# One core, attention and experts over 32 sequences: producers moved ahead in each slot, value matmuls in two bursts, values and gates in one float32 matmul, a straight program for the first sequences

## The chip, the cores and the metric

The kernel runs on one core of a Trainium2 chip. The core has five engines that run their own programs side by side and wait for each other on semaphores: TensorE (PE; its weight load is PEld), VectorE (DVE), ScalarE (ACT), GpSimd (POOL) and SyncE (SP), which here issues every DMA. The metric is the device time of one launch in microseconds (us). A run is called by its median over several executions; the profile is one further execution.

## The reference

`x` is 32 sequences of 256 tokens with 128 features. The result is `x + attention(layernorm(x)) + experts(layernorm(x))`.

```
xn = (x - mean) / sqrt(var + 1e-5)
q, k, v = xn @ Wq.T + bq, xn @ Wk.T + bk, xn @ Wv.T + bv      # 16 heads of 8 features
scores = q k^T / sqrt(8), causal;  attn = softmax(scores);  a = (attn v) @ Wo.T + bo
logits = xn @ gate_w.T                                        # 8 experts
top 2 of 8, softmax of the two logits; y = sum of the two experts xn @ We[e], weighted
out = x + a + y
```

## The kernel before

The unit of work is one sequence. The work on a sequence is spread over six slots of the program. Slot `s` holds, in every engine's program, the work of several sequences at once, each at another stage: sequence `s+3` (`NXT`) is normalised, turned by TensorE and split into a high and a low half in `fp32r`; sequence `s+2` (`PRE`) is projected to q and k, and each of these is split into three bf16 parts; sequence `s` has its scores taken; sequence `s-1` has its transposed scores, exponentials and experts; sequence `s-2` is finished. Each slot has 12 items `n` (`ITEMS`); each item is one 128x512 block of scores of sequence `s` on TensorE, whose row maxima VectorE takes (`take_max`, L589), and one 128x512 block of transposed scores (`scoreT_item`) of the sequence that is one slot behind for n of 4 and more (`LAG`), two behind for n under 4, whose exponentials ScalarE takes (L473). Both have two PSUM buffers: block n waits for the reader of block n-2.

The three bf16 parts travel over DRAM: SP writes them to `scratch` (L305 to L309) and loads them back as rows of `qstack` and `kstack` (L323, L327), 1.2 MB a sequence in six DMAs. The row maxima travel too: TensorE turns them (L914), ScalarE and VectorE split them (L518, L633, `mT`), and SP writes them as two rows of `qstack` (L299). The first transposed block of a sequence, at n = 4 of the next slot, waits for these two rows (`dma_max`). The other rows of a stack are constants (`q_steps`, `k_steps`), filled once for each of the four buffers by VectorE (L737) and ScalarE (L554).

Values and gates: `m1 = xnT.T @ wvg` at n = 0, as four products of halves for each of the two 128-token tiles (`by_halves(..., whole=True)`, eight matmuls of 136 columns). Experts: four blocks of three matmuls with 512 columns (L779), at n = 4, 6, 8 and 10, in two PSUM tiles `m1` and `m2`, read by VectorE (`lower`, L626) and ScalarE (`upper`, L508). Attention values (`values`, L847): four groups a sequence, at n = 9 and 11 of slot `s+1` and n = 3 and 5 of slot `s+2`, from two `probs` buffers. An fp32 matmul stands in the trace as two records.

The order of the work is written out by hand, by `if n == ...` in each engine's `slot`. `over_slots` runs slots -3 to 3 straight, 4 to 27 in a loop of four, and the rest straight; `between(s)` is what the start does between two slots (filling constants, splitting weights). SP issues its DMAs in program order, and a wait holds back all that stands behind it.

Of the kernel before, what the change touches and what calls it, by code (L numbers as in the profile page):

```python
# [33 lines left out]
E = 8  # L34
# [80 lines left out]
def bass_block(nc, x, wq, wk, bq, bk, wv, bv, wo, bo, gate, we, out):  # L115
    ctx = ExitStack()
    with ctx:
# [12 lines left out]
        def sems(*names):  # L130
# [8 lines left out]
        wvg_hl = sb("wvg_hl", [P, 2, VG], FP32R)  # L139
# [6 lines left out]
        ident_b = sb("ident_b", [P, P], BF16)  # L146
# [8 lines left out]
        xb = sbs("xb", [P, QT, D])  # L155
        xnT_hl = sbs("xnT_hl", [P, 2, S], FP32R)
# [6 lines left out]
        probs = sbs("probs", [P, 3, HG, P], n=2)  # L163
# [8 lines left out]
        wvg_high = sb("wvg_high", [P, VG])  # L172
# [38 lines left out]
        ld_qk, ld_w, ld_we, ld_bias, pool_const, dve_const, pe_bias, dve_bias = sems(  # L211
            "ld_qk", "ld_w", "ld_we", "ld_bias", "pool_const", "dve_const", "pe_bias", "dve_bias")
# [8 lines left out]
        pe_xnT, dve_halves, act_high, pool_xb = sems("pe_xnT", "dve_halves", "act_high", "pool_xb")  # L221
# [11 lines left out]
        NQK, NW, CONSTS = 4, 4, 8  # L233
# [6 lines left out]
        def over_slots(eng_fori, slot, between=None):  # L240

            for s in range(-NXT, LOOP0):
                slot(Seq(0, s), s)
                if between:
                    between(s)
# [19 lines left out]
        def _(sp):  # L265
# [3 lines left out]
            sp.dma_start(bqk_sb[:, 0:1], bq.unsqueeze(1)).then_inc(ld_qk, 16)  # L269
            sp.dma_start(bqk_sb[:, 1:2], bk.unsqueeze(1)).then_inc(ld_qk, 16)  # L270
            sp.dma_start(wvg_sb[:, 0:D], wv).then_inc(ld_w, 16)
            sp.dma_start(wvg_sb[:, D:VG], gate).then_inc(ld_w, 16)
            sp.dma_start(wo_sb[:], wo).then_inc(ld_w, 16)
            sp.dma_start(bv_sb[:], bv.unsqueeze(1)).then_inc(ld_w, 16)
            sp.dma_start(bias_out[:], bo.unsqueeze(0).to_broadcast([P, D])).then_inc(ld_bias, 16)
# [7 lines left out]

            def slot(t, s):
                if has(s, -3):
                    store(t + (-3))
                if has(s, NXT) and s > -NXT:
                    nxt = t + NXT
                    sp.wait_ge(pool_xn, upto(nxt + (-NB)))
                    sp.wait_ge(pool_xb, upto(nxt + (-NB)))  # L290
                    sp.dma_start(x_sb[nxt.buf][:], x_t[nxt.n]).then_inc(dma_x[nxt.buf], 16)
                if s == -2:
                    sp.dma_start(we_sb[:], we.rearrange("e d m -> d e m")).then_inc(ld_we, 16)
# [705 lines left out]
```

## Time and profile before

| | us |
|---|---|
| three runs, median (lowest, highest) | 561.86 (561.7, 562.83) |
| the profiled execution, its own time | 564.58 |
| its span, first to last instruction | 562.8 |
| PE busy | 516.0 |
| DVE busy | 439.1 |
| ACT busy | 400.9 |
| POOL busy | 346.4 |

The span splits in three: a start up to the first full slot, thirty slots of nearly one length, and a tail in which no new sequence comes. Busy PE is not PE at its peak; the chain of waits shows the distance from one piece of PE work to the next. The granted TensorE clock stands in tenths of full speed; its mean over the execution is 0.993.

### The profile page before, as it was taken

The numbers are of one execution on the slowest core, as the hardware profiler recorded it, in microseconds if no ns is written. First come the engines' busy times: TensorE is split into PE (matmuls) and PEld (weight loads), VectorE is DVE, ScalarE is ACT, GpSimd is POOL, SyncE is SP. The second block draws the span as 40 slices with busy tenths as digits, with TensorE's granted clock in tenths as the row PEclk, the third lists the DMA queues.
The fourth block names the chain that finished last, engine by engine and source line by source line (L and its number), as shares of the span: only waits on it lengthen the run. The fifth ranks groups of instructions, "written<-read, shape, count | busy, mean of one in ns | idle before, by whom it ended". The sixth has DMA issues, their size and how long they took to land.

```text
span 562.8 us, 19500 instructions
## 1 busy us (share of the span) xinstructions
PE 516.0 (92%) x6402; PEld 402.3 (71%) x6402; DVE 439.1 (78%) x1109; ACT 400.9 (71%) x1033; POOL 346.4 (62%) x565
## 2 busy tenths in 40 slices
PE   1157999999999999999999999999999999999986
PEld 1145777777777777777777787777777778777754
DVE  3268888888888888888888888888888888877721
ACT  5624677777777777778777777777877777776664
POOL 4323576666666777666666677766666667754433
PEclk9999999999999999999999999999999999999988
DMA  3645555464455555544544555554445455540000
GB/s 98 172 98 139 137 138 137 110 145 125 110 132 137 145 137 135 134 130 120 128 128 117 137 145 136 131 139 126 128 118 133 115 139 147 137 130 12 12 12 20
DMA packets 64002, 67.11 MB, mean 119 GB/s; under 512 B 6752, under 2 KB 59104, under 8 KB 59104
## 3 DMA queue, kind: packets, MB, share of 16 engines
q1 hardware_dynamic: 63968, 66.68, 47.0%
q8 instruction: 19, 0.31, 0.2%
q14 instruction: 15, 0.12, 0.1%
HBM read 44.90 MB, written 21.23 MB: 118 GB/s over the span
## 4 chain that ended last, share of the span: by engine, by line
PE 79%; ACT 7%; DMA 4%; issue 4%; DVE 3%; POOL 2%; SPq 1%; ACTq 1%; POOLq 0%; DVEq 0%
PE m L779 26%; PE oT_ps L847 14%; PE scoreT_ps L823 10%; PE score_ps L803 9%; PE scoreT_ps L828 6%; PE score_ps L797 4%; ACT probs L473 3%; PE m L956 3%; DMA qstack<-mT 2%; PE m L951 2%; ACT parts L496 2%; PE m L893 1%; PE m L925 1%; DMA x_sb<-in_x 1%; PE m L914 1%
## 5 line engine op out<-in xcount | busy, mean ns | idle before, releaser
L589 DVE TENSOR_REDUCE negmax<-score_ps 128x2 f32<-128x512 f32 (+1 forms) x384 | 260.4, 686 | 51.9 <-PE score_ps L803 37.8
L473 ACT ACTIVATE probs<-scoreT_ps 128x512 f32<-128x512 f32 x384 | 225.8, 607 | 88.7 <-PE scoreT_ps L823 44.5
L779 PE MATMUL m<-we_hl,xnT_hl 128*128 128x512 f32 x384 | 122.9, 429 | 0.0
L847 PE MATMUL oT_ps<-probs,vaug 128*32 128x256 f32 (+1 forms) x2048 | 110.2, 333 | 0.0
L823 PE MATMUL scoreT_ps<-qstack,kstack 123*128 123x128 bf16 (+1 forms) x1024 | 102.7, 222 | 5.1 <-DMA qstack<-mT 4.5
L803 PE MATMUL score_ps<-kstack,qstack 72*128 72x128 bf16 (+1 forms) x1024 | 104.3, 224 | 1.9 <-DVE negmax L589 1.8
L372 POOL TENSOR_TENSOR fours<-lower,upper 128x512 f32<-128x512 f32 x64 | 81.8, 1278 | 22.1 <-ACT upper L508 21.3
L823 PEld LDWEIGHTS scoreT_ps<-qstack,kstack 123*128 123x128 bf16 (+1 forms) x1024 | 68.3, 98 | 33.1 <-issue 21.6
L366 POOL TENSOR_TENSOR parts<-rest,parts 128x256 bf16<-128x256 f32 x64 | 41.9, 673 | 72.0 <-ACT parts L501 71.6
L847 PEld LDWEIGHTS oT_ps<-probs,vaug 128*32 128x32 f32 x2048 | 53.6, 109 | 37.6 <-issue 5.4
L803 PEld LDWEIGHTS score_ps<-kstack,qstack 72*128 72x128 bf16 (+1 forms) x1024 | 71.1, 100 | 5.6 <-DVE negmax L589 3.8
L508 ACT ACTIVATE upper<-m,weight 128x128 f32<-128x128 f32 x256 | 73.5, 381 | 0.0
L779 PEld LDWEIGHTS m<-we_hl,xnT_hl 128*128 128x128 f32 x384 | 63.8, 193 | 5.7
L432 POOL TENSOR_SCALAR xn<-x_sb,mv,rstd 128x128 f32<-128x128 f32 x64 | 51.0, 802 | 8.1 <-POOL rstd L427 8.1
L828 PE MATMUL scoreT_ps<-qstack,kstack 123*128 123x128 bf16 x512 | 50.9, 222 | 3.6 <-ACT probs L473 1.8
L797 PE MATMUL score_ps<-kstack,qstack 123*128 123x128 bf16 x512 | 51.5, 224 | 0.5 <-DVE negmax L589 0.5
L828 PEld LDWEIGHTS scoreT_ps<-qstack,kstack 123*128 123x128 bf16 x512 | 29.2, 98 | 27.2 <-issue 15.0
L379 POOL TENSOR_TENSOR gap<-top 128x2 f32<-128x2 f32 x32 | 6.3, 196 | 66.6 <-DVE top L598 66.6
L626 DVE TENSOR_TENSOR lower<-m,weight 128x512 f32<-128x512 f32 x64 | 43.6, 681 | 4.7 <-PE m L779 4.7
L496 ACT ACTIVATE parts<-m,bqk_sb 128x256 bf16<-128x256 f32 x64 | 26.9, 471 | 22.4 <-PE m L779 22.4
L416 POOL TENSOR_TENSOR pairs<-fours 128x512 f32<-128x512 f32 x32 | 41.0, 1283 | 0.2
L797 PEld LDWEIGHTS score_ps<-kstack,qstack 123*128 123x128 bf16 x512 | 35.5, 100 | 7.5 <-DVE negmax L589 7.0
(82 smaller groups left out, 696.6 us busy)
## 6 DMA issues: line engine op xcount, KB each, us to landing
kstack<-scratch SPq DMA_DIRECT2D x96, 192.0 KB
scratch<-parts SPq DMA_DIRECT2D x64, 192.0 KB, 2.4
qstack<-scratch SPq DMA_DIRECT2D x64, 192.0 KB
qstack<-scratch SPq DMA_DIRECT2D x32, 256.0 KB
x_sb<-in_x SPq DMA_DIRECT2D x32, 128.0 KB, 2.1
scratch<-parts SPq DMA_DIRECT2D x32, 128.0 KB, 1.9
out<-out_sb SPq DMA_DIRECT2D x32, 128.0 KB, 1.9
qstack<-mT SPq DMA_DIRECT2D x64, 8.0 KB, 1.8
```

The costliest lines, as they stand in the source:

```text
L372: g.tensor_tensor(fours[:, :, q, :], lower[:, :, q, :], upper[:, :, q, :], ALU.add).then_inc(pool_sum, 1)
L432: ins = g.tensor_scalar(xn[:, q, :], x_sb[nxt.buf][:, q, :], mv[:, q, 0:1], rstd[:, q:q + 1], ALU.subtract, ALU.mult)
L473: a.activation(o, i, ACT.Exp, scale=SCALE).then_inc(act_exp, 1)
L508: ins = a.activation(upper[:, e, q, :], m2[:, e * D:(e + 1) * D], ACT.Copy, scale=weight[m.buf][:, q, EH + e:EH + e + 1])
L589: v.tensor_reduce(o, score_ps[n % 2][:].rearrange("p (h k) -> p h k", h=w), axis=AX.X, op=ALU.max, negate=True).then_inc(dve_max, 1)
L626: v.tensor_tensor(lower[:, :, q, :], m1[:].rearrange("p (e m) -> p e m", e=EH), weight[m.buf][:, q, 0:EH].unsqueeze(2).to_broadcast([P, EH ...
L779: ins = tn.matmul(o, l, r, start=i == 0, stop=i == len(products) - 1)
L797: ins = tn.matmul(ps[:, c * P:(c + 1) * P], qs[0:ALL_ROWS, h, 0:P], ks[0:ALL_ROWS, h, 0:P], start=True, stop=True)
L803: ins = tn.matmul(ps[:, c * S + q * P:c * S + (q + 1) * P], qs[0:top, h, P:S], ks[0:top, h, q * P:(q + 1) * P], start=True, stop=True)
L823: ins = tn.matmul(ps[:, c * S + q * P:c * S + (q + 1) * P], ks[0:top, h, 0:P], qs[0:top, h, q * P:(q + 1) * P], start=True, stop=True)
L828: ins = tn.matmul(ps[:, c * P:(c + 1) * P], ks[0:ALL_ROWS, h, P:S], qs[0:ALL_ROWS, h, P:S], start=True, stop=True)
L847: ins = tn.matmul(o, va[:, q, h, :], i, start=q == 0 and grp % VGRP == 0, stop=q == 1 and grp % VGRP == VGRP - 1, skip_group_check=True)
```

## The change

The following changes, and nothing else:

- Values and gates become one fp32 matmul for each 128-token tile, from a plain fp32 copy `xnT` of the turned input. ScalarE makes this copy (`copy_input`) before VectorE splits the same PSUM tile. The split of `wvg` goes.
- The four groups of attention values move: groups 0 and 1 together at n = 3 of slot `s+2`, groups 2 and 3 together at n = 6. `probs` has four buffers for it.
- Expert blocks 0 and 1 stand together at n = 4, block 2 at n = 9, block 3 at n = 11. Values and gates move from n = 0 to n = 1.
- Many pieces on ACT, DVE and POOL change their item: the row statistics of `s+3` from n = 6 and 7 to n = 1 and 2, `xn` from 7 to 5, `oT` from 5 to 6, `part1` from n = 1 to 2, the two `upper` blocks in front of the item's exponential or behind it.
- SP loads the input four slots ahead, and behind the maxima instead of ahead of them.
- Slots -3 to -1 are replaced by a straight program for sequences 0 to 2 on each engine; x of the first four sequences is loaded at once. `ident_b`, which nothing read, goes.
- The constants of the stacks: `kstack` 0 is filled by VectorE, `kstack` 1 by ScalarE ahead of slot 0, `kstack` 2 and 3 behind slots 0 and 1. The experts' weights are split behind slot 0 instead of ahead of it.

```diff
+            for s in range(LOOP0):
                 slot(Seq(0, s), s)
                 if between:
...
+            sp.dma_start(x_sb[1][:], x_t[1]).then_inc(dma_x[1], 16)
+            sp.dma_start(bqk_sb[:, 0:1], bq.unsqueeze(1)).then_inc(ld_bqk, 16)
+            sp.dma_start(bqk_sb[:, 1:2], bk.unsqueeze(1)).then_inc(ld_bqk, 16)
...
+            sp.dma_start(bv_sb[:], bv.unsqueeze(1)).then_inc(ld_w, 16)
+            sp.dma_start(wo_sb[:], wo).then_inc(ld_w, 16)
+            sp.dma_start(x_sb[2][:], x_t[2]).then_inc(dma_x[2], 16)
+            sp.dma_start(wvg_sb[:, 0:D], wv).then_inc(ld_w, 16)
+            sp.dma_start(wvg_sb[:, D:VG], gate).then_inc(ld_w, 16)
+            sp.dma_start(bias_out[:], bo.unsqueeze(0).to_broadcast([P, D])).then_inc(ld_bias, 16)
+            sp.dma_start(we_sb[:], we.rearrange("e d m -> d e m")).then_inc(ld_we, 16)
+            sp.dma_start(x_sb[3][:], x_t[3]).then_inc(dma_x[3], 16)
...
+                if s + PRE < NB:
+
+                    sp.wait_ge(dve_stack, s + PRE + 2)
+                    sp.wait_ge(act_stack, s + PRE)
+                    sp.wait_ge(ld_zero, 16 * NB)
...
+                if has(s, NB):
+                    new = t + NB
+                    sp.wait_ge(pool_xn, upto(t))
+                    sp.wait_ge(pool_xb, upto(t))
+                    sp.dma_start(x_sb[new.buf][:], x_t[new.n]).then_inc(dma_x[new.buf], 16)
...
+            for s in range(-PRE, 0):
+                stacks(Seq(0, s + PRE), s)
...
+            normalise(Seq(0, 0))
+            mask_steps()
+            normalise(Seq(0, 1))
+            part3(Seq(0, 0))
+            normalise(Seq(0, 2))
+            part3(Seq(0, 1))
...
+                    act.wait_ge(pe_pv, upto(f + (-1), per=NG, k=grp + 1))
...
+            def copy_input(nxt):
+                act.wait_ge(pe_xnT, upto(nxt))
+                a.copy(xnT[nxt.buf][:], m1[:, 0:S]).then_inc(act_xnT, 1)
...
+                    if n == 11 and has(s, NXT):
+                        copy_input(t + NXT)
                     if n == 11 and has(s, -1):
-                        upper_experts(t + (-1), 1)
+                        upper_experts(mix, 1)
+                    if n == 11 and has(s, NXT):
...
             def between(s):
-                if s < NB - NXT:
-                    if s == -NXT:
-                        act.wait_ge(pool_steps, 2 * STEPS + 1)
-                    fill_keys(s + NXT)
-                if s == -1:
+                if s == 0:
                     act.wait_ge(dve_weights, 3)
-                    a.copy(wvg_hl[:, 0], wvg_high[:]).then_inc(act_weights, 1)
-                    act.wait_ge(dve_weights, 5)
                     a.copy(we_hl[:, 0], w_high[:]).then_inc(act_weights, 1)
+                if s < 2:
+                    fill_keys(s + 2)
...
+            copy_input(Seq(0, 0))
+            round_input(Seq(0, 0))
+            act.wait_ge(ld_bqk, 16 * 2)
+            part1(Seq(0, 0))
+            part2(Seq(0, 0))
+            copy_input(Seq(0, 1))
+            round_input(Seq(0, 1))
+            part1(Seq(0, 1))
+            part2(Seq(0, 1))
+            copy_input(Seq(0, 2))
+            round_input(Seq(0, 2))
+            act.wait_ge(pool_steps, 2 * STEPS + 1)
+            fill_keys(1)
             over_slots(act.Fori, slot, between)
 
...
+            fill_stack(qstack[0], q_steps)
+            fill_stack(kstack[0], k_steps)
+            take_rest(Seq(0, 1))
+            fill_stack(qstack[1], q_steps)
+            dve.wait_ge(pe_bias, 1)
...
-            def by_halves(o, high, low, other_high, other_low, whole=False):
-
-
-                products = [(high, other_high), (high, other_low), (low, other_high)] + [(low, other_low)] * whole
-                for i, (l, r) in enumerate(products):
-                    ins = tn.matmul(o, l, r, start=i == 0, stop=i == len(products) - 1)
+            def by_halves(o, high, low, other_high, other_low):
...
-                            ins = by_halves(m1[:, q * VG:(q + 1) * VG], xnT_hl[t.buf][:, 0, q * P:(q + 1) * P],
-                                            xnT_hl[t.buf][:, 1, q * P:(q + 1) * P], wvg_hl[:, 0], wvg_hl[:, 1], whole=True)
+                            ins = tn.matmul(m1[:, q * VG:(q + 1) * VG], xnT[t.buf][:, q * P:(q + 1) * P], wvg_sb[:],
+                                            start=True, stop=True)
...
-                    if n == 7 and has(s, -2):
+                        project(pre)
+                    if n == 3 and has(s, -2):
+                        values(fin, 0)
+                        values(fin, 1)
+                    if n == 4 and has(s, -1):
+                        if s == 1:
+                            pe.wait_ge(dve_weights, 4)
+                            pe.wait_ge(act_weights, 2)
+                        if has(s, 0):
+                            pe.wait_ge(act_v, upto(t))
+                        else:
+                            pe.wait_ge(dve_lower, upto(fin, per=2))
+                        experts(mix, 0)
+                        if has(s, PRE):
+                            pe.wait_ge(dve_rest, upto(pre, per=2))
+                        else:
+                            pe.wait_ge(act_upper, upto(fin, per=2))
+                        experts(mix, 1)
+                    if n == 6 and has(s, -2):
+                        values(fin, 2)
+                        values(fin, 3)
+                    if n == 8 and has(s, -2):
                         pe.wait_ge(act_oT, upto(fin))
...
+                    if n == 9 and has(s, -1):
+                        pe.wait_ge(dve_lower, upto(mix, per=2, k=1))
+                        experts(mix, 2)
...
+                    if n == 11 and has(s, -1):
+                        pe.wait_ge(act_upper, upto(mix, per=2, k=1))
+                        experts(mix, 3)
...
+            pe.wait_ge(pool_const, 5)
+            turn_input(Seq(0, 0))
+            pe.wait_ge(dve_weights, 2)
+            pe.wait_ge(act_weights, 1)
+            project(Seq(0, 0))
+            pe.wait_ge(dve_halves, 2)
+            turn_input(Seq(0, 1))
+            pe.wait_ge(ld_w, 16 * NW)
+            pe.wait_ge(dve_const, 1)
+            tn.matmul(m0[:, 0:D], bv_wide[:], wo_sb[:], start=True, stop=True).then_inc(pe_bias, 1)
+            project(Seq(0, 1))
+            pe.wait_ge(dve_halves, 4)
+            turn_input(Seq(0, 2))
+            over_slots(pe.Fori, slot, between=None)
 
```

TensorE, slot 2 before, from score block 3 to score block 6 (`score_ps` scores, `scoreT_ps` transposed scores, `oT_ps` attention values, `we_hl` experts):

```order
L797 MATMUL score_ps<-kstack,qstack 128x128 x4
L847 MATMUL oT_ps<-probs,vaug 32x256 x4
L847 MATMUL oT_ps<-probs,vaug 32x128 x4
L828 MATMUL scoreT_ps<-qstack,kstack 128x128 x4
L803 MATMUL score_ps<-kstack,qstack 128x128 x4
L779 MATMUL m<-we_hl,xnT_hl 128x512 x3
L823 MATMUL scoreT_ps<-qstack,kstack 128x128 x4
L803 MATMUL score_ps<-kstack,qstack 128x128 x4
L823 MATMUL scoreT_ps<-qstack,kstack 128x128 x4
L847 MATMUL oT_ps<-probs,vaug 32x256 x4
L847 MATMUL oT_ps<-probs,vaug 32x128 x4
L797 MATMUL score_ps<-kstack,qstack 128x128 x4
```

The same slot in the changed kernel, from score block 3 to the transposed block of n = 4:

```order
L829 MATMUL score_ps<-kstack,qstack 128x128 x4
L879 MATMUL oT_ps<-probs,vaug 32x256 x4
L879 MATMUL oT_ps<-probs,vaug 32x128 x4
L879 MATMUL oT_ps<-probs,vaug 32x256 x4
L879 MATMUL oT_ps<-probs,vaug 32x128 x4
L860 MATMUL scoreT_ps<-qstack,kstack 128x128 x4
L835 MATMUL score_ps<-kstack,qstack 128x128 x4
L811 MATMUL m<-we_hl,xnT_hl 128x512 x6
L855 MATMUL scoreT_ps<-qstack,kstack 128x128 x4
```

Two groups of values now stand between one score block and the next, and two expert blocks between the next two.

ScalarE, the end of slot 0 and the start of slot 1 in the changed kernel (`kstack<-k_steps` fills constants, `mT` is the split of the maxima, which SP sends on):

```order
L519 CAST xnT_hl<-xnT_high 128x256
L575 CAST we_hl<-w_high 128x1024
L569 COPY kstack<-k_steps 64x4096
L486 COPY logits<-m 128x16
L496 COPY vaug<-m 128x8x2x8 x2
L538 CAST mT<-m 16x256
```

The same place before:

```order
L554 COPY kstack<-k_steps 64x4096
L525 CAST xnT_hl<-xnT_high 128x256
L478 COPY logits<-m 128x16
L488 COPY vaug<-m 128x8x2x8 x2
L518 CAST mT<-m 16x256
```

The cast of the experts' weights and the fill of `kstack` 2 come between the last work of slot 0 and the maxima of sequence 0.

SyncE, slots 0 and 1 in the changed kernel (the loads of stack 2, the maxima of sequence 0, the input of sequence 5, the first parts of sequence 3):

```order
L309 DMA qstack<-scratch 24x4096 x2
L309 DMA qstack<-scratch 32x4096
L313 DMA kstack<-scratch 24x4096 x3
L324 DMA qstack<-mT 1x16x256 x2
L329 DMA x_sb<-in_x 128x2x128
L291 DMA scratch<-parts 128x2x256
```

The same place before:

```order
L323 DMA qstack<-scratch 24x4096 x2
L323 DMA qstack<-scratch 32x4096
L327 DMA kstack<-scratch 24x4096 x3
L291 DMA x_sb<-in_x 128x2x128
L299 DMA qstack<-mT 1x16x256 x2
L305 DMA scratch<-parts 128x2x256
```

Only the input moved behind the maxima. In both kernels the maxima of sequence 0 stand behind the loads of stack 2, and these wait for the fill of `kstack` 2. That fill stood before slot 0; now it is the one behind slot 0 on ScalarE.

## Rows read from the trace of the kernel before

**Rows 1.** The page: busy time by engine; the chain of waits by engine.

```profile
PE 516.0 (92%) x6402; PEld 402.3 (71%) x6402; DVE 439.1 (78%) x1109; ACT 400.9 (71%) x1033; POOL 346.4 (62%) x565
...
PE 79%; ACT 7%; DMA 4%; issue 4%; DVE 3%; POOL 2%; SPq 1%; ACTq 1%; POOLq 0%; DVEq 0%
```

**Rows 2.** Stretches: length, busy us of each engine, granted clock, DMA share, GB/s.

```profile
208.70:224.30 15.60, 15.52 (x202) 12.23 (x202) 13.29 (x35) 11.88 (x33) 10.69 (x18) 1.00 0.53 137
...
223.30:224.30 1.00, 1.00 (x14) 0.99 (x13) 0.53 (x2) 1.00 (x4) 0.79 (x2) 1.00 0.73 172
224.30:225.30 1.00, 1.00 (x13) 1.00 (x13) 0.85 (x2) 0.48 (x3) 1.00 (x1) 1.00 0.01 0
```

**Rows 3.** Chain of waits in one steady slot: start us, us, what.

```profile
208.45 0.23 PE score_ps L797 x4
208.67 0.90 PE m L779 x8
...
212.30 0.50 ACT probs L473
...
212.84 0.40 PE scoreT_ps L828 x4
...
214.48 0.23 PE score_ps L803 x4
...
214.94 0.79 PE oT_ps L847 x16
215.73 0.33 PE score_ps L797 x4
...
223.56 0.50 PE m L956 x4
224.06 0.22 PE score_ps L797 x4
```

**Rows 4.** Groups of instructions: busy us, mean ns, idle before and its releaser.

```profile
L589 DVE TENSOR_REDUCE negmax<-score_ps 128x2 f32<-128x512 f32 (+1 forms) x384 | 260.4, 686 | 51.9 <-PE score_ps L803 37.8 <-PE score_ps L797 8.2 <-issue 0.2
...
L554 ACT COPY kstack<-k_steps 64x4096 bf16<-64x4096 bf16 x4 | 14.4, 3602 | 0.1
...
L548 ACT COPY oTn<-m 128x256 f32<-128x256 f32 x32 | 11.7, 367 | 2.5 <-PE m L925 2.5
...
L737 DVE COPY qstack<-q_steps 64x4096 bf16<-64x4096 bf16 x4 | 4.9, 1224 | 0.1
...
L566 ACT CAST we_hl<-w_high 128x1024 fp32r<-128x1024 f32 x1 | 1.0, 1047 | 2.3 <-DVE w_high L643 2.3
```

**Rows 5.** Who waited for whom: us in total, times, longest.

```profile
PE scoreT_ps L823 <- DMA qstack<-mT: 4.5, 6, 1.3
PEld scoreT_ps L823 <- DMA qstack<-mT: 4.2, 13, 0.8
```

**Rows 6.** DMA issues: KB each, median us from issue to landing.

```profile
qstack<-mT SPq DMA_DIRECT2D x64, 8.0 KB, 1.8
```

**Rows 7.** Chain of waits at the start: an input issued behind six stack loads.

```profile
19.50 6.91 DMA x_sb<-in_x
```

**Rows 8.** Timeline of PE at the start (slot 0, slot 1, slot 2).

```profile
34.78 0.63 PE L797 MATMUL score_ps<-kstack,qstack 123*128 123x128 bf16 x4
...
57.16 0.65 PE L823 MATMUL scoreT_ps<-qstack,kstack 123*128 123x128 bf16 x4
...
66.44 0.39 PE L797 MATMUL score_ps<-kstack,qstack 123*128 123x128 bf16 x4
```

**Rows 9.** Timeline of DVE at the start (slot 0, slot 1).

```profile
37.33 1.28 DVE L589 TENSOR_REDUCE negmax<-score_ps 128x4 f32<-128x512 f32 x2
...
53.73 0.41 DVE L633 TENSOR_TENSOR mT<-m,mT 16x256 bf16<-16x256 f32 x1
```

**Rows 10.** Timeline of PE in the tail.

```profile
541.90 1.63 PE L779 MATMUL m<-we_hl,xnT_hl 128*128 128x512 f32 x3
...
545.47 0.95 PE L779 MATMUL m<-we_hl,xnT_hl 128*128 128x512 f32 x3
```

More of the change, by code:

```diff
@@ L446, in slot @@
                                         bias_out[:].unsqueeze(1).to_broadcast([P, QT, D]), ALU.add).then_inc(pool_xb, 1)
-                    if n == 10 and has(s, -1):
-                        sum_tile(t + (-1), 0)
+                    if n == 0 and has(s, -2):
+                        sum_tile(fin, 1)
+                    if n == 1 and has(s, -2):
+                        pool.wait_ge(pool_sum, upto(fin, per=RESULT, k=SUM_Q1))
+                        g.tensor_tensor(pairs[:], fours[:, 0:2], fours[:, 2:4], ALU.add).then_inc(pool_sum, 1)
@@ new lines, in slot @@
+                    if n == 2 and has(s, 0):
+                        gates(t, GAP)
+                    if n == 3 and has(s, -2):
+                        pool.wait_ge(pool_sum, upto(fin, per=RESULT, k=PAIRS))
+                        g.tensor_tensor(mixed[:], pairs[:, 0], pairs[:, 1], ALU.add).then_inc(pool_sum, 1)
+                    if n == 4 and has(s, PRE):
+                        part3(t + PRE)
+                    if n == 5 and has(s, -2):
+                        pool.wait_ge(pool_sum, upto(fin, per=RESULT, k=FOURS))
+                        pool.wait_ge(pool_xb, upto(fin))
+                        pool.wait_ge(dve_out, upto(fin + (-1)))
+                        g.tensor_tensor(res[:], mixed[:], xb[fin.buf][:], ALU.add).then_inc(pool_sum, 1)
@@ L667, in slot @@
+                    if n == 2 and has(s, 0):
                         best_experts(t)
                     if n == 2 and has(s, PRE):
[L669 to L674 removed]
+                        take_rest(t + PRE)
@@ L957, in slot @@
                         ins.then_inc(pe_y, 1)
-            def between(s):
-                if s == -1:
-                    pe.wait_ge(ld_w, 16 * NW)
-                    pe.wait_ge(dve_const, 1)
-                    tn.matmul(m0[:, 0:D], bv_wide[:], wo_sb[:], start=True, stop=True).then_inc(pe_bias, 1)
-            EXPERT_STEPS = (4, 6, 8, 10)
-            pe.wait_ge(pool_const, CONSTS + 2)
-            over_slots(pe.Fori, slot, between)
+                    if f:
+                        scoreT_item(f, k)
+                    if n == 10 and has(s, -2):
+                        pe.wait_ge(dve_o, upto(fin))
+                        for q in range(QT):
+                            ins = tn.transpose(m0[:, q * P:(q + 1) * P], o_sb[:, q, :], ident[:])
+                        ins.then_inc(pe_oTn, 1)
+            pe.wait_ge(pool_const, 5)
[12 more added lines that the diff above has]
+            over_slots(pe.Fori, slot, between=None)
 def kernel(L0_attn_x, L0_attn_Wq, L0_attn_bq, L0_attn_Wk, L0_attn_bk, L0_attn_Wv, L0_attn_bv,
```

491 lines of the change are left out of this document (210 added, 281 removed).

## The prediction

> **What bounds the kernel.** I read the page first: PE is busy for 92% of the span and makes 79% of the chain of waits [rows 1]. Then the stretches: in one steady slot PE is busy for 15.52 of 15.60 us, DVE for 13.29, ACT for 11.88, POOL for 10.69, at granted clock 1.00, the 2.4 GHz level [rows 2]. A busy PE may still stall inside, so I read the chain of one slot piece by piece. From score block 0 at 208.45 to the next slot's at 224.06 are 15.61 us, and the pieces follow each other with nothing between, save one place where the chain passes through an exponential at 212.30 and a transposed block takes 0.40 us instead of 0.24, a wait of some 0.15 us [rows 3]. So in thirty of the slots time is the sum of PE's pieces, and the change is worth there what it takes from that sum, as long as no other engine takes over. At the start PE mostly waits; what counts there is when each sequence's first piece can run, which the timelines tell [rows 7 to 9].
>
> **Values and gates.** Eight matmuls take 0.90 us of the chain from 208.67 [rows 3]. The two fp32 ones become four records of 136 columns. The nearest row is L956, four records of 128 columns: 0.50 us [rows 3], so 0.50 x 136/128 = 0.53, a gain of 0.37 us a slot. Best bound: four records at the pace of a 128-column score matmul (0.23/4) would take 0.25, gain 0.65. Worst: weight loads that are not hidden, 0.9 us or more, gain 0. I take 0.53, since L956 has the same types and nearly the same shape.
>
> The Trainium skill, Perfetto Trace Analysis (the table of engine rates), halves TensorE's output rate for FP32_LOW_HIGH, and its page TensorE: Matmul & The Clock Gate (weight-path perf modes) gives the fast weight load only to types other than FP32. By the rate alone four records of 136 columns would take 4 x 136 x 2 / 2.4 GHz = 0.45 us as an estimate; the L956 row gives 0.50 for 128, so the trace is a bit slower than that rule, and a penalty on the weight load, if there is one, is already in that row.
>
> **Bursts.** A score block costs 0.23 us of the chain, but 0.33 behind a group of values (215.73 against 214.48) [rows 3]. Four groups pay this before, two pairs now: gain 2 x 0.10 = 0.20 us a slot, between 0 (each group pays it by itself) and 0.35 (the entry into a group is cheaper too).
>
> **Pieces further from their producers.** The 0.15 us wait for the exponential behind `part1` should go. Blocks of transposed scores also wait for the maxima that come by DMA: 4.5 + 4.2 = 8.7 us in 19 waits [rows 5]. Experts 0 and 1 and the first pair of values now lie ahead of the block that waits, so it comes some 0.7 us later behind its producer than before. Of the 8.7 us I count 2.0 as gained in the steady part; PE and PEld may show one wait twice. The next slot's maxima go out about 0.9 us after the six loads of a stack are through; before, those loads end at about 224.3, where the DMA share falls from 0.73 to 0.01 [rows 2], so there is still room, but little.
>
> **What the cover must hold.** I added the engines' pieces in the new order over one slot. ACT gets one copy more, 0.37 us (like L548) [rows 4]: 12.3 of 15.0 us. DVE keeps its 13.3, so it may idle 1.7 us a slot. At four places the reader of a PE tile or its producer is within 0.1 us of being late: exponential 6 for block 8 (it stands behind `oT`), `oT` for its transposes, the lower experts' product for the turned input, `o_sb` for its transposes. I take 0.15 us a slot for these together. Zero is possible, and 0.5 if each of them pays 0.1 and drags the next.
>
> Slot: 0.37 + 0.20 + 0.15 - 0.15 = 0.57 us, 15.61 to 15.04. Thirty slots: 17.1, with the maxima 19.1 us.
>
> **The start.** The straight program has stack 0 ready to load at about 17.7 us, set by DVE, which now fills both its constants, 2 x 1.22 us [rows 4]. Loads take some 8 us. Before, score block 0 nevertheless came at 34.78 [rows 8], since the third input landed only 6.91 us after it was issued at 19.50, behind the six loads [rows 7], and weights were split ahead of the first row maxima at 37.33 [rows 9]. Now inputs are there early: score block 0 at about 26. That is 8.8 us ahead. But much of it is given back. DVE's slot 0 (10.5 us as before, and the `q` fill and the experts' weights behind it, 4 us) ends at 43. ACT waits for those weights, casts them (1.05) and fills `kstack` 2 (3.60) [rows 4], to 46.6. Then come the maxima of sequence 0: `mT` at 48 against 53.73 [rows 9]. The loads of stack 2 wait for the same fill and are issued from 46.7 to 49.0; SP issues the maxima only behind them. A DMA of maxima lands in 1.8 us [rows 6], but directly behind six loads an input took 6.91 [rows 7]. So the maxima land at about 55, and the first transposed block, with both expert blocks done, runs there. Before, it ran at 57.16 with one expert block still to come (1.4 us at the low clock) [rows 8]: 58.6 against 55.2, 3.4 us gained. The two groups of values that leave slot 1 give 1.6 more; a later warm-up of PE takes 1.0. Slot 1 ends 4.0 us ahead (66.44 [rows 8] becomes 62.4).
>
> Slot 2: `kstack` 3 is filled behind slot 1, 3.60 us on ACT [rows 4], when exponentials are due. ACT's queue behind it: an exponential, the logits, the maxima, `part1`. The fill ends 5.1 us into the slot; stack 3's six loads wait for it, and the maxima of sequence 1 stand behind them: they land at 5.1 + 8.5 = 13.6 us, where PE wants them at 6.9. That is 6.7 us of stall. In the tail before, three expert matmuls took 1.63 us behind such waits against 0.95 elsewhere [rows 10], so PE's clock falls back; I add 1.5 us. Loss in slot 2: 8.2. Start in sum: 4.0 - 8.2 = -4.2 us, a loss. Bounds: the maxima overtake the loads and the clock holds, +4.3; both stalls 2 us longer, -8.
>
> The Trainium skill, TensorE: Matmul & The Clock Gate (HAM oscillation), says that a long enough idle stretch throttles TensorE again; the tail row agrees with it.
>
> **The tail.** Values of the last sequence, two groups, move to after its last blocks: +2.1 us. The expert pair and the first pair of values fill the wait for the last maxima: -2.2. In sum 0, within 2 either way.
>
> **Sum.** 19.1 - 4.2 = 14.9 us. The profiled execution took 564.58 us, which becomes 549.7. The median of the runs is 561.86, 2.7 below; with the same saving it becomes 547.0.
>
> **Rivals.**
> 1. The maxima are not held by the loads (they share the queues fairly). For it: steady maxima land in 1.8 us while other traffic runs [rows 6]. Against it: the 6.91 us of [rows 7]. The start then gains 4.3: 561.86 - 19.1 - 4.3 = 538.5.
> 2. The near ties all pay: 0.5 us a slot in place of 0.15, and the maxima's 2 us are not gained. 547.0 + 30 x 0.35 = 557.5. For it: the bursts, 1.7 us in which no block comes, use up the two-buffer cushion. Against it: DVE idles 51.9 us before its maxima now [rows 4], so there is some slack.
> 3. DVE becomes the bound: slower. Mechanism: TensorE delivers score blocks in clumps. During each of the four bursts (two pairs of values, the expert pair, expert block 3 with the output product) DVE runs dry for 0.7 us, and its work cannot be made up. 13.3 us of DVE work plus 2.8 = 16.1 a slot, 0.5 more than now: 561.86 + 15 + 4.2 = 581. It decides once DVE idles more than 15.6 - 13.3 = 2.3 us a slot, which is just what it idles now [rows 2]. Against it: the present idle is time in which DVE waits for PE, not a need.
> 4. No gain: the fp32 matmuls cost the 0.90 of the eight and the bursts pay per group. The start's loss and small gains cancel: about 561.
>
> **Chances.** Forecast 0.55, with 542 to 551.5 as its own range. Rival 1 0.16, rival 2 0.18, rival 3 0.06, rival 4 0.05. The range 537 to 556.5 holds nearly all of the forecast, most of rival 1 and half of rival 2. A measurement of this kernel tells about 0.2% (1.1 us) from no change. Faster by more: 0.55 + 0.16 + 0.17 + 0.02 = 0.90; the same 0.03; slower 0.07.
>
> **What would show it.** Steady pitch of score block 0 at 15.04 us, values and gates 0.53, one 0.33 piece behind each pair of values. First row maxima near 27 us. The fill of `kstack` 2 ending near 46.6 and the first transposed block at about 55. In slot 2, a PE wait of over 5 us for `qstack<-mT`. Wrong if the pitch is over 15.3 (a near tie pays: the waits name which), if the maxima in slots 1 and 2 land in 2 us behind the loads, or if score block 0 is not before 30 us.

## The result, and the profile after

The kernel after takes 582.7 us (median of 4 runs, 576.1 to 588.3) against 562.35 beside it on the same chip: ratio 1.032, 95% interval 1.023 to 1.041. The run of 588.3 fell in a slower state and is left out of the ratio. The kernel is slower; forecast were 547.0 us, within 537.0 to 556.5, with a chance of 0.90 for faster. The profiled execution took 584.07 us, with a span of 582.3.

Its page, first the busy times, the granted clock of the 40 slices, the instruction queues and the chain by engine:

```profile
PE 499.8 (86%) x6274; PEld 408.2 (70%) x6274; DVE 426.1 (73%) x1108; ACT 403.3 (69%) x1063; POOL 349.0 (60%) x563
...
PEclk9965869999979999699988999699996999999999
...
q8 instruction: 64, 1.05, 0.8%
q14 instruction: 40, 0.33, 0.2%
...
PE 74%; issue 8%; DMA 6%; ACT 4%; DVE 4%; SPq 2%; POOL 1%; ACTq 0%; POOLq 0%; DVEq 0%
```

PE is busy for 16 us less than in [rows 1], yet the span is 19.5 us longer. "issue", time in which an engine waits for nothing that the profile shows, has 8% of the chain where [rows 1] have 4%, and the clock falls at regular places. In the kernel before q8 moved 19 packets and q14 15.

The steady slot answers to [rows 2, 3]. Windows (length, busy us of PE, PEld, DVE, ACT, POOL, granted clock, DMA share, GB/s), and some of the chain's pieces (start us, us, what):

```profile
138.39:152.85 14.46, 14.46 (x200) 12.05 (x204) 12.77 (x35) 12.02 (x34) 10.67 (x18) 1.00 0.56 138
...
229.60:234.63 5.03, 0.00 (x0) 0.00 (x1) 0.47 (x2) 1.37 (x5) 2.52 (x2) 0.79 0.42 91
235.88:238.08 2.20, 0.00 (x0) 0.00 (x1) 0.09 (x1) 0.42 (x1) 0.00 (x0) 0.50 0.00 0
238.08:244.93 6.85, 6.85 (x71) 5.86 (x72) 3.94 (x12) 2.89 (x9) 0.88 (x2) 0.66 0.09 25
```

```profile
138.39 1.44 PE oT_ps L879 x32
139.83 0.33 PE scoreT_ps L860 x4
...
150.47 0.52 PE m L919 x4
```

An undisturbed slot takes 14.46 us, less than the forecast 15.04. All of it is PE at the 2.4 GHz level. Values and gates take 0.52 us, a pair of values 1.44 and the block behind it 0.33. The windows below it show a disturbed slot. PE does nothing for 5.03 us, in which the others run out of work (POOL is still busy for 2.52 us, ACT for 1.37), and again for 2.20 us, in which all are nearly idle (ACT 0.42, DVE 0.09). Then come 6.85 us at a granted clock of 0.66, partly at the 1.2 GHz level. The chain shows this pattern five times, always ahead of score block 0 of the slot to which the loop branches back (slots 4 to 27 are six passes of four slots, so five branches back). These are its pieces "issue" of over 1 us, and below them PE's own waits (us in total, times, longest):

```profile
164.24 2.77 issue
167.75 2.40 issue
...
229.60 5.03 issue
235.88 2.20 issue
...
297.69 5.43 issue
304.36 1.92 issue
...
366.38 4.56 issue
372.18 1.62 issue
...
433.76 5.23 issue
440.24 1.64 issue
```

```profile
PE score_ps L829 <- issue: 23.0, 5, 5.4
...
PE score_ps L835 <- issue: 9.8, 5, 2.4
```

The start answers to [rows 8, 9]. Timelines of PE and of DVE, in brackets the wait:

```profile
27.12 0.59 PE L829 MATMUL score_ps<-kstack,qstack 123*128 123x128 bf16 x4 [6.87 <-DMA kstack<-scratch]
...
57.59 0.59 PE L855 MATMUL scoreT_ps<-qstack,kstack 123*128 123x128 bf16 x4 [4.53 <-DMA qstack<-mT]
...
64.91 0.39 PE L829 MATMUL score_ps<-kstack,qstack 123*128 123x128 bf16 x4
...
80.42 0.58 PE L855 MATMUL scoreT_ps<-qstack,kstack 123*128 123x128 bf16 x4 [3.66 <-DMA qstack<-mT]
```

```profile
27.74 1.29 DVE L612 TENSOR_REDUCE negmax<-score_ps 128x4 f32<-128x512 f32 x2 [4.83 <-PE score_ps L829]
...
48.72 0.41 DVE L707 TENSOR_TENSOR mT<-m,mT 16x256 bf16<-16x256 f32 x1 [2.65 <-ACT mT L538]
```

The chain of waits over the same time shows what the forecast named, the fills and the maxima behind them:

```profile
44.32 3.61 ACT kstack L569
...
51.03 6.43 DMA qstack<-mT
...
66.82 3.61 ACT kstack L569
...
73.75 6.53 DMA qstack<-mT
...
95.00 3.12 DMA qstack<-mT
```

Where the 19.5 us of span went can be read from the chain: values and gates of slot 4 start at 98.43 before and at 106.95 after (where they stand one score block and one transposed block, 0.45 us, later in the slot), those of slot 31 at 521.20 and at 545.63. So the start lost 8.1 us, the 27 slots between lost 438.7 - 422.8 = 15.9 us, and the end gained 4.5. At 14.46 a slot the 27 would have taken 390.4: the stalls cost 48 us and turned a gain of 32 into this loss.

### The profile page after: what moved, and what is told of

It is laid out like the page before. It is cut to its first block, busy times and chain, and to the rows that moved or that the text cites. A ratio compares the mean times of both kernels' runs of the same rounds, so it can differ in the third digit from the quotient of the medians.

```text
span 582.3 us, 19332 instructions
## 1 busy us (share of the span) xinstructions
PE 499.8 (86%) x6274; PEld 408.2 (70%) x6274; DVE 426.1 (73%) x1108; ACT 403.3 (69%) x1063; POOL 349.0 (60%) x563
## 3 DMA queue, kind: packets, MB, share of 16 engines
q8 instruction: 64, 1.05, 0.8%
## 4 chain that ended last, share of the span: by engine, by line
PE 74%; issue 8%; DMA 6%; ACT 4%; DVE 4%; SPq 2%; POOL 1%; ACTq 0%; POOLq 0%; DVEq 0%
PE m L811 18%; PE oT_ps L879 15%; PE scoreT_ps L855 10%; PE score_ps L835 10%; PE scoreT_ps L860 6%; PE score_ps L829 5%; DMA qstack<-mT 4%; PE m L919 3%; PE m L962 2%; PE m L980 2%; PE m L894 2%; DVE negmax L612 1%; ACT upper L526 1%; ACT kstack L569 1%; PE m L987 1%
## 5 line engine op out<-in xcount | busy, mean ns | idle before, releaser
L612 DVE TENSOR_REDUCE negmax<-score_ps 128x2 f32<-128x512 f32 (+1 forms) x384 | 251.1, 678 | 99.1 <-PE score_ps L835 70.1
L481 ACT ACTIVATE probs<-scoreT_ps 128x512 f32<-128x512 f32 x384 | 218.7, 603 | 115.9 <-PE scoreT_ps L860 64.7
L835 PE MATMUL score_ps<-kstack,qstack 72*128 72x128 bf16 (+1 forms) x1024 | 107.8, 228 | 19.4 <-issue 9.8
L811 PE MATMUL m<-we_hl,xnT_hl 128*128 128x512 f32 x384 | 114.7, 421 | 0.0
L879 PE MATMUL oT_ps<-probs,vaug 128*32 128x256 f32 (+1 forms) x2048 | 99.5, 336 | 0.0
L835 PEld LDWEIGHTS score_ps<-kstack,qstack 72*128 72x128 bf16 (+1 forms) x1024 | 74.3, 102 | 23.5 <-DVE negmax L612 11.9
L855 PEld LDWEIGHTS scoreT_ps<-qstack,kstack 123*128 123x128 bf16 (+1 forms) x1024 | 72.1, 101 | 26.1 <-issue 17.1
L879 PEld LDWEIGHTS oT_ps<-probs,vaug 128*32 128x32 f32 x2048 | 58.4, 112 | 30.7 <-issue 3.2
L811 PEld LDWEIGHTS m<-we_hl,xnT_hl 128*128 128x128 f32 x384 | 66.2, 193 | 8.8
L811 PE MATMUL m<-xnT_hl,wqk_hl 128*128 128x256 f32 x192 | 36.6, 336 | 2.6 <-DVE xnT_hl L665 2.6
```

The costliest lines, as they stand in the source:

```text
L481: a.activation(o, i, ACT.Exp, scale=SCALE).then_inc(act_exp, 1)
L612: v.tensor_reduce(o, score_ps[n % 2][:].rearrange("p (h k) -> p h k", h=w), axis=AX.X, op=ALU.max, negate=True).then_inc(dve_max, 1)
L811: ins = tn.matmul(o, l, r, start=first, stop=l is low)
L835: ins = tn.matmul(ps[:, c * S + q * P:c * S + (q + 1) * P], qs[0:top, h, P:S], ks[0:top, h, q * P:(q + 1) * P], start=True, stop=True)
L855: ins = tn.matmul(ps[:, c * S + q * P:c * S + (q + 1) * P], ks[0:top, h, 0:P], qs[0:top, h, q * P:(q + 1) * P], start=True, stop=True)
L879: ins = tn.matmul(o, va[:, q, h, :], i, start=q == 0 and grp % VGRP == 0, stop=q == 1 and grp % VGRP == VGRP - 1, skip_group_check=True)
```

## The experiments

Theory: the stall is TensorE's own program being loaded again at each branch back. Counted in the built programs, in blocks of 256 instructions from the program's start (each matmul and each transpose is a weight load and a matmul; an fp32 matmul is twice that). ScalarE's program stands below with its own experiments.

```
TensorE        loop begins at  instructions of four slots  blocks of 256 touched  q8 packets
before         1287            1709                        7                      19
after          1195            1678                        8                      64
```

The change made the loop 31 instructions shorter and what stands ahead of it 92 shorter, and the second moved the loop over one more block. 64 - 19 = 45 packets are nine for each of five branches back. A packet of q8 is 1.05 MB / 64 = 16 KB, one of q14 0.33 MB / 40 = 8 KB. The whole program before has 4979 instructions, 19.4 blocks of 256: its 19 packets are the program read once.

The Trainium skill, Runtime: NRT & Kernel Launch (Instruction fetch mechanics), states a buffer of 2048 instructions for TensorE, refilled in blocks of 16 KiB or 256 instructions, and says that "Branching breaks sequential prefetch". The same section has a branch stall when its target is not in a window of two blocks ("2-page window"). By that rule the kernel before, whose loop is 1709 instructions long, would stall as well; its 19 packets say that it doesn't, and here the measurement decides. The size of q8's packets agrees with the blocks; q14's are half of that, so there the run decides, and I count 128 instructions for a packet of it. Seven blocks of 256 are within 2048, and eight would just fill it; that seven stay and eight don't is what the runs below show, and the page doesn't say it.

**TensorE's program moved in the kernel after (94 increments).** Nobody waits for the semaphores `pe_passed` and, further down, `sp_passed`; the increments only take up room in the program.

```diff
+            for _ in range(94):
+                pe.sem_inc(pe_passed, 1)
             over_slots(pe.Fori, slot, between=None)
```

> The kernel after, with 94 semaphore increments ahead of TensorE's loop and nothing else: its program of 1678 instructions for four slots then begins 9 instructions behind a multiple of 256 instead of 171, and lies on 7 blocks of 256 instructions and not on 8. Theory (the five stalls at the loop's back edge are TensorE's instructions loaded again, since the loop doesn't fit the blocks that stay): no stall there, the pitch stays at 14.46 us, the instruction queue q8 falls from 64 packets to 19; five times 7.5 to 10.3 us go, so 582.7 - 49 = about 534 us. Rival (the stalls come from data: a semaphore, a late transfer, another engine's program): the stalls stay, 582 us.

Measured: 563.0 us (559.3 to 566.6, ratio to before 1.0025, interval 0.998 to 1.007). 19.7 us less than after, with nothing changed inside a slot, and q8 at 19 packets; but not 534. The chain and the waits of this run name two rests. The increments themselves cost 7.2 us ahead of slot 0 (they take 13.8 us for 94, and PE had waited only 6.9 us there), and another engine now stood still at each branch back. Chain:

```profile
26.79 7.16 issue
...
170.29 5.28 issue
234.93 3.02 issue
296.93 3.30 issue
358.00 2.85 issue
419.81 3.61 issue
```

Who waited for what (us in total, times, longest), ACT and then PE of the same kernel:

```profile
ACT probs L481 <- issue: 18.6, 5, 5.4
...
PE score_ps L829 <- issue: 13.8, 1, 13.8
```

PE has no such wait at a branch any more, ACT has five. In the kernel after, with TensorE's stalls over them, ACT's showed only once (3.2 us). Here q14 still has 40 packets, against 15 in the kernel before: 25 more, five for each branch back.

**The kernel before, moved the other way.**

```diff
+            for _ in range(164):
+                pe.sem_inc(pe_passed, 1)
             over_slots(pe.Fori, slot, between)
```

> The kernel before, with 164 semaphore increments ahead of TensorE's loop: its loop of 1709 instructions, which lay on 7 blocks of 256, then lies on 8, with nothing changed inside a slot. Theory: five or six stalls at the back edge appear that the kernel before never had, q8 goes from 19 to about 64 packets, 562 + 5 x 8 to 10 = 602 to 612 us. Rival (something that the change did inside a slot causes the stalls): no stall, 562 us.

Measured: 626.7 us, ratio 1.117 (1.113 to 1.120); q8 65 packets, q14 15. Some of it is the increments, which stand ahead of everything that the loop's first slots need here: the chain has "issue" of 22.0 us at 8.49. The rest, 65 - 22 = 43 us, I put down to the branches back. Pieces of its chain:

```profile
253.28 3.99 issue
258.61 1.42 issue
...
324.35 4.08 issue
330.54 1.20 issue
```

The same pair as in the kernel after, in a kernel whose slots are untouched, and 71.1 us apart where four slots before took 62.5: 8.6 us for this branch back, and five times that is 43. So nothing in the slots' new order is needed for the stalls.

**More increments, still eight blocks.** As in the first experiment, with 216 increments in place of 94.

> The kernel after, with 216 semaphore increments ahead of TensorE's loop, more than twice as many as in the run with 94, but so that the loop still lies on 8 blocks of 256. Theory: the stalls stay, 582 us within 4. Rival (it is the increments themselves, as a delay ahead of the loop, that take the stalls away): as the run with 94 of them, 534 us.

Measured: 598.1 us (591.5 to 602.8); q8 65 packets. The time was missed by 16 us, since I had counted the increments as free: its chain has "issue" of 26.25 us at 26.86 ahead of slot 0. The question it was made for is answered: the five stalls are there (3.9 to 6.5 us each in the chain), so it is the position that matters and not the increments.

**ScalarE's program moved as well.** Its loop of four slots has 275 instructions (269 before) and begins 7 later than before, at 179.

```diff
         def _(act):
             a = nc.scalar
+            for _ in range(25):
+                act.sem_inc(sp_passed, 1)
...
+            for _ in range(46):
+                pe.sem_inc(pe_passed, 1)
             pe.wait_ge(pool_const, 5)
...
+            for _ in range(48):
+                pe.sem_inc(pe_passed, 1)
             over_slots(pe.Fori, slot, between=None)
```

> The kernel after, with 94 increments on TensorE again, but 46 of them at the very start and 48 ahead of slot 0, where TensorE waited 6.9 us anyway in the kernel after, and 25 increments at the start of ScalarE's program. In the run with all 94 ahead of slot 0 the chain showed a wait of 7.2 us for them, and ScalarE, not TensorE, stood still once per four slots (5 waits, 18.6 us), with 40 packets in instruction queue q14 as in the kernel after and 15 in the kernel before. Theory (ScalarE's loop of 275 instructions has come to lie over one block of 128 more than before; the 25 put it on three again): q8 19 packets, q14 15 packets, no stall at the back edge, 563.0 - 7.2 - 5 x 4.5 = 533 us within 3. Rival (ScalarE's stall has another cause): q14 stays at 40, 563.0 - 7.2 = 556 us.

Measured: 534.6 us (534.05 to 534.88), ratio 0.952 (0.949 to 0.955). The instruction queues are those of the kernel before, and no wait of over 1 us stands at a branch back:

```profile
q8 instruction: 19, 0.31, 0.2%
q14 instruction: 15, 0.12, 0.1%
```

582.7 - 534.6 = 48.1 us, which is what the stalls had cost by the chain. This is the kernel that the forecast was about.

That ScalarE's stall went with the 25 increments shows that the position decides there too. It doesn't show the "three blocks" of the expectation: counted from the program's start the loop lies on three blocks of 128 in the kernel before (it begins at 172), after (179) and here (204) alike. Three that stay and four that don't come out only if some 61 to 70 further instructions stand ahead of the program, which no run shows. For TensorE's seven and eight blocks up to 71 further instructions would change nothing.

**ScalarE alone, in the kernel before.**

```diff
         def _(act):
             a = nc.scalar
+            for _ in range(13):
+                act.sem_inc(sp_passed, 1)
```

> The kernel before with 13 semaphore increments at the start of ScalarE's program, as many as the change adds there ahead of the loop's end, and nothing else; TensorE's program is untouched. Theory (a multiple of 128 now falls before the end of ScalarE's loop): q14 goes from 15 to 40 packets, q8 stays at 19, ScalarE waits 3 to 5 us for nothing visible at each of five back edges, and 5 x 4.5 us are added: 562 + 22 = 584 us within 5. Rival: 562 us, since 13 increments at the start cost nothing.

Measured: 587.0 us, ratio 1.045 (1.040 to 1.050); q8 19, q14 40. Thirteen instructions at the start of an engine that isn't the bottleneck cost 25 us, and since nothing else differs, the 25 further packets of q14 are ScalarE's. Its waits:

```profile
ACT xnT_hl L527 <- issue: 14.2, 5, 3.8
...
ACT vaug L490 <- issue: 6.4, 5, 1.4
```

**ScalarE alone, in the kernel after.** Only the 25 increments.

> The kernel after with the 25 increments at the start of ScalarE's program and none on TensorE: ScalarE's loop fits, TensorE's doesn't. Expected q8 64 packets, q14 15. TensorE alone cost 65 - 22 = 43 us in the kernel before when shifted, ScalarE alone 25 us there; both together cost 582.7 - 534.6 = 48 us in the kernel after. Theory (the two are loaded at the same time and the longer one counts): 576 to 581 us. Rival (they add up; ScalarE's share of 21 us goes): 561 us.

Measured: 581.7 us (579.7 to 585.1); q8 64, q14 15. That is the kernel after within its spread: the two engines' stalls run beside each other and the longer one counts. Mending ScalarE alone shows 1 us, mending TensorE alone 19.7 (26.9 without the 7.2 us of its increments), and both 48.1.

**The start changed.** The 94 increments ahead of slot 0, and:

```diff
-                    sp.wait_ge(dve_stack, s + PRE + 2)
-                    sp.wait_ge(act_stack, s + PRE)
+                    sp.wait_ge(dve_stack, (2, 3, 5, 7)[s + PRE])
+                    sp.wait_ge(act_stack, min(s + PRE, 1))
...
-                if s < 2:
-                    fill_keys(s + 2)
...
-                if s < 2:
-                    fill_stack(qstack[s + 2], q_steps)
+                if s == 0:
+                    fill_stack(qstack[3], q_steps)
...
             halve_input(Seq(0, 2))
+            fill_stack(qstack[2], q_steps)
+            fill_stack(kstack[2], k_steps)
+            fill_stack(kstack[3], k_steps)
             over_slots(dve.Fori, slot, between)
```

> The run with 94 increments, and the start changed as well: the constants of qstack 2 and of kstack 2 and 3 are filled on VectorE ahead of slot 0 and no longer on ScalarE and VectorE behind slots 0 and 1, and that of qstack 3 behind slot 0. Theory (the loss at the start is the maxima of sequences 0 and 1, which stand in SyncE's queue behind six loads each, and these behind the 3.6 us fills): stack 2 loads early, the maxima land 2 us after their issue; against the run with 94 increments alone some 3 us less in slots 0 and 1 (the three fills cost VectorE 3 to 4 us ahead of its first maxima) and 6 to 8 us less in slot 2, and with the clock kept about 519 to 526 us against 534. Rival (the transfers are slow because the DMA engines are full, whatever the order): within 2 us of the run with 94 increments.

Measured: 545.5 us (543.8 to 550.5) against 563.0 without the new start, 17.5 us less (expected: 8 to 15). The absolute time (519 to 526) was missed, since it was reckoned from 534 and the run with 94 increments took 563.0.

**Both loops fit, and the start changed.**

> As the run in which both loops fit, with the changed start (constants of qstack 2, kstack 2 and 3 on VectorE ahead of slot 0). That start took 563.0 to 545.5 us beside the stalls, 17.5 us. Theory (the two are independent): 533 - 17.5 = 516 us. Rival (the 7.2 us of increments ahead of slot 0 had given VectorE the time for its fills, and without them score block 0 waits for them): 519 to 522 us.

Measured: 516.7 us (515.7 to 520.2), ratio to before 0.922 (0.918 to 0.927): 17.9 us below 534.6, so the two are independent. It is the fastest version of this study. Its timelines of SyncE and of DVE show why:

```profile
38.36 1.11 SPq L309 DMA_DIRECT2D qstack<-scratch  x3
39.51 1.19 SPq L313 DMA_DIRECT2D kstack<-scratch  x3
46.64 1.25 SPq L324 DMA_DIRECT2D qstack<-mT  x2
```

```profile
25.55 1.22 DVE L756 COPY kstack<-k_steps 64x4096 bf16<-64x4096 bf16 x1
...
46.22 0.40 DVE L707 TENSOR_TENSOR mT<-m,mT 16x256 bf16<-16x256 f32 x1
```

Stack 2's loads have all been issued by 40.7 us, 6 us ahead of the maxima of sequence 0; in the kernel after the two stand directly behind each other. The chain has no wait of over 0.5 us for `qstack<-mT` before 89.88. The same constant of `kstack` takes 1.22 us on DVE and 3.60 on ACT [rows 4]. The mean granted clock over the span is 0.994 in the profiled execution, against 0.965 where only the loops fit; over all executions it is 0.977 to 0.994 against 0.961 to 0.980.

**Values and gates in halves again.** On the kernel in which both loops fit (with 18 increments in place of 48 ahead of slot 0, for the same seven blocks).

```diff
+                        other = wqk_hl[:].rearrange("p h c d -> p h (c d)")
                         for q in range(QT):
-                            ins = tn.matmul(m1[:, q * VG:(q + 1) * VG], xnT[t.buf][:, q * P:(q + 1) * P], wvg_sb[:],
-                                            start=True, stop=True)
+                            o = m1[:, q * VG:(q + 1) * VG]
+                            x = [xnT_hl[t.buf][:, h, q * P:(q + 1) * P] for h in range(2)]
+                            tn.matmul(o, x[0], other[:, 0, 0:VG], start=True, stop=False)
+                            tn.matmul(o, x[0], other[:, 1, 0:VG], start=False, stop=False)
+                            tn.matmul(o, x[1], other[:, 0, 0:VG], start=False, stop=False)
+                            ins = tn.matmul(o, x[1], other[:, 1, 0:VG], start=False, stop=True)
```

> As the run in which both loops fit, but values and gates are computed with eight matmuls of halves as in the kernel before (with the halves of the query weights as stand-in, so the values and gates are those of other weights). Predicted gain of this part 0.37 us a slot; in the kernel after the four fp32 matmuls take 0.52 us. Theory (TensorE's pieces add up in a slot): 0.38 us a slot come back, 30 x 0.38 = 11 us over the run without it, about 544 us. Rival (another engine sets the pitch by now): within 2 us of it.

Measured: 545.5 us (544.7 to 546.3), 10.9 more; the pitch of its slots is 14.83 us against 14.47, and 30 x 0.36 = 10.8. TensorE's sum still sets the slot.

**Values one group at a time.**

```diff
-                    if n == 3 and has(s, -2):
-                        values(fin, 0)
-                        values(fin, 1)
+                    if n in (2, 3) and has(s, -2):
+                        values(fin, n - 2)
...
-                    if n == 6 and has(s, -2):
-                        values(fin, 2)
-                        values(fin, 3)
+                    if n in (5, 6) and has(s, -2):
+                        values(fin, n - 3)
```

> As the run in which both loops fit (534.6 us), with the four groups of values of a slot one by one at items 2, 3, 5 and 6 instead of in two pairs. Predicted price of this part: 0.20 us a slot, 6 us. The trace of after gives more: a pair takes 1.44 us and its next block 0.33, two single groups took 0.79 each and two blocks 0.33 [rows 3], so (1.58 + 0.66) - (1.44 + 0.56) = 0.24 a pair, 0.48 a slot, 30 x 0.48 = 14 us: about 549 us. Rival (the order at items 2 and 5 makes something else late, or covers it): over 555, or within 2 us of 534.6.

Measured: 559.1 us (557.9 to 561.1), 24.5 more, in the rival's range (over 555) and not the theory's: the pitch is 15.30, 0.83 us above 14.47, and something else does come late. Part of its chain:

```profile
265.34 0.79 PE oT_ps L881 x16
...
266.99 0.59 ACT upper L528 x2
...
267.99 0.62 ACT oT L546
...
268.66 0.66 PE m L962 x4
```

0.48 of the 0.83 is what the pieces say. In the other 0.35 the chain leaves PE behind the last group and passes over ACT: an exponential, two products of an expert block, then the copy `oT`, which comes too late for its transposes at L962. PE waits for it 31 times (6.0 us in total), where the kernel with pairs does so twice (1.2 us). So the pairs save an entry each and, in this order, also keep that near tie from paying. Why ACT is behind with single groups stays open.

**Expert blocks one at a time.**

```diff
                         experts(mix, 0)
...
+                    if n == 5 and has(s, -1):
                         experts(mix, 1)
```

> As the run in which both loops fit, with expert block 1 an item behind expert block 0 and not directly behind it. Theory (an expert block of 512 columns pays little for its entry: a pair takes 1.45 us, a single one 0.70 to 0.76): within 0.07 us a slot, 534.6 to 537 us. Rival (each entry costs what a group of values pays, 0.1 to 0.24): 538 to 542 us.

Measured: 542.1 us (541.0 to 544.0), 7.4 more, in the rival's range, but not by the rival's mechanism. The pitch is 14.54 us, 0.07 more, as the theory has it: some 2 us in all. Most of the rest lies in slots that wait for maxima: PE waits 13.7 us for `qstack<-mT` in 5 waits, against 9.3 in 2. The pair of experts is work ahead of the block that waits.

## Why the prediction was wrong

**The step that failed** is the sentence that in thirty of the slots "time is the sum of PE's pieces", with the forecast made as thirty equal slots. Every fourth slot also holds the branch back of a loop, which cost nothing visible in the kernel before, and I took that for a property of the loop. It was one of where its instructions lay. No rival had it; the only slower one, DVE as the bound (0.06, 581 us), came to nearly the right number by a mechanism that isn't there: DVE is busy for 12.77 of 14.46 us and PE never stops for it. The runs show in its place: TensorE's loop, over eight blocks and not seven, is loaded again at each of five branches back, ScalarE's loop has moved to a place where it is too, and both together cost 48.1 us. The page of before carried the count that I didn't read, 19 packets in q8 for a program that branches back five times, and the order of instructions showed how many left the part ahead of the loop.

**Values and gates** (0.37 forecast): 0.36 a slot by the experiment, 10.9 us. Right, from the L956 row.

**Bursts** (0.20): too small. Going back costs 0.83, 0.48 of it in the pieces. I priced only the slower block behind a group (0.10) and not the entry of the group itself: two groups took 2 x 0.79, a pair takes 1.44.

**Waits and near ties** (0.15 against 0.15): the chain of a steady slot has no wait left, so the near ties cost nothing as they stand, and rival 2 falls. (Its 557.5 also left out the 2.0 us of the maxima that it takes as not gained; with them it would be 559.5.) That they are near shows in the run with single groups, where the one at `oT`'s transposes costs up to 0.35.

**Pitch** 14.46 instead of 15.04. It was undersized by 0.58, 17 us over thirty slots: 0.28 are the bursts' pieces and 0.15 the near ties that cost nothing; the remaining 0.15 no run splits. The 2.0 us for maxima in the steady part were at most 1.3: before, the 27 slots from 98.43 to 521.20 took 15.66 us on average and an undisturbed one 15.61.

**The start**: the mechanism was right, the size was not. Score block 0 came at 27.12 (26 forecast), `mT` of sequence 0 at 48.72 (48), the first transposed block at 57.59 (55), so that slot 1 ended at 64.91 and not 62.4. In slot 2 the transfer of the maxima takes 6.53 us in the chain. PE's wait for it is 3.66, under the 5 us named as a sign; with 1.65 behind the row maxima and 1.40 behind ACT's exponential, which stands behind the fill, PE is idle for 6.7 us there, as forecast. The clock costs more than the 1.5 us put down for it: from 80.4 to 91.4 us it is 0.76, and the pair of values there takes 2.79 us, not 1.44. In sum the start lost 8.1 us until slot 4, not 4.2: some 2.5 of the difference is slot 1, the rest the slower clock in slot 2 and a transfer of maxima of 3.1 us in the chain of slot 3 that I hadn't foreseen (PE waits 0.64 for it). The run with the new start takes the whole of it away and more (17.9 us), and behind the loads the maxima took 6.43 and 6.53 us, so rival 1, that the loads don't hold the maxima, falls as well.

**The tail** (0, within 2): the end, from slot 31's values and gates, gained 4.5 us. 1.1 of it is slot 31's share of the shorter pitch, the other 3.4 are more than was forecast; no run takes them apart.

**Sum**: 547.0 was forecast, 534.6 is what the change gives without the stalls. The signs and mechanisms of its terms held, but in sum they were 12 us short of the gain: even without the stalls the time would have lain below the range of 537.0 to 556.5. The omitted term of 48 us turned the sign.

## What to carry to other kernels

When a kernel loops, count where each engine's loop lies and how many instruction blocks it touches, before and after a change: instructions added or removed ahead of the loop, on any engine, move it as well as those within. The page's instruction queues tell at once: here packets that grew by a fixed number per branch back (nine, five) were a program loaded again; "issue" in the chain at the branch is the price. Such a stall on one engine can hide another's, so look at every engine before judging a change's worth, and judge the rest of the change only with the loops at rest.

## What was not expected of the hardware

- Seven blocks of 256 instructions of TensorE's loop stayed (19 packets; the kernel before, the kernel after once moved, and its variants with other slots); eight did not (64 or 65 packets): nine packets for each branch back, and 7.5 to 10.4 us in the kernel after (each stretch of four slots with a stall, less 4 x 14.46). For ScalarE a shift of 13 instructions was enough: five packets of 8 KB for each branch back, on average 5.1 us in the kernel before (25.4 / 5) and 4.2 in the kernel after with TensorE's loop moved ((563.0 - 7.2 - 534.6) / 5).
- About a third of the price is the slow work behind the stall: of 48.3 us PE stands for 32.8 (23.0 + 9.8). The clock had fallen by then. It is 0.50 from 238.08 to 242.00 and 0.66 over the whole 6.85 us, and values and gates behind the first stall take 1.01 us instead of 0.52.
- A semaphore increment on TensorE isn't free: 94 of them in a row took 13.8 us, 147 ns each, and 216 took 32.7, 151 ns each.
- What lies exactly at the edge between seven blocks and eight, and whether further instructions stand ahead of a program on the chip, weren't measured.
